# Audio tower on one core: the layer norms' epsilon kept as a 129th column beside the squares, in place of an addition on GpSimd

## The chip, the cores and the metric

The kernel runs on one NeuronCore of one Trainium2 chip, as one program. The metric is the device time of one execution in microseconds; three runs of the kernel before gave 622.33, 622.41 and 625.29, a median of 622.41.

## The reference, cut to what matters

64 recordings of 4000 samples go through seven 1-D convolutions (10 taps with stride 5; four with 3 taps and two with 2 taps, all stride 2), each with 128 channels, a layer norm over the channels and an exact Gelu. A last layer norm and a projection to 192 columns give 12 tokens a recording; attention and a feed-forward part with nine experts follow, each behind a layer norm.

```python
def _fp32_layernorm(x, g, b, eps=1e-05):
    xf = x.astype(jnp.float32)
    mu = xf.mean(-1, keepdims=True)
    var = xf.var(-1, keepdims=True)
    y = (xf - mu) * jax.lax.rsqrt(var + eps) * g.astype(jnp.float32) + b.astype(jnp.float32)
    return y.astype(x.dtype)

h = x[:, None, :]
for w, g, b, s in zip(conv_ws, ln_gs, ln_bs, strides):
    h = _conv1d(h, w, s)
    h = jnp.swapaxes(h, -2, -1)
    h = _fp32_layernorm(h, g, b)
    h = jnp.swapaxes(h, -2, -1)
    h = jax.nn.gelu(h, approximate=False)
```

## The kernel before

The recordings are worked in eight groups of eight (g = 0 to 7). Layers 1 to 6 are cut into 128 blocks ("chunks") of 1 to 4 tiles; a tile is up to 128 positions (partitions) by C = 128 channels (columns), so a full block is 128 x 512 in one PSUM bank. The taps are centred beforehand, so a convolution's output has mean zero over the channels, and the norm needs only the sum of its squares. For block n this is done:

- `conv` (L750, TensorE): the convolution into PSUM bank n mod 3. It waits until the product of block n-3 is done (`xh_done`) and for the Gelus that make its input.
- `square` (L1361, ScalarE): the squares of the block into `sq`, one of two halves of 512 columns of the tile `work`.
- `group` on VectorE (L1080): `ssum`, the sum over each run of 128 columns.
- `group` on GpSimd (L599, L602): `varv` = `ssum` + C times eps, then `rstd` = `varv` to the power -0.5. A semaphore (`varv_done`) stands between the two.
- `norm` (L1090, VectorE): `xh`, in the second half of `work`, is the block in PSUM times `rstd`.
- `turn` (L762, TensorE): transposes of `xh` into one PSUM bank, `tr`, which has to be free of the Gelu before.
- `gelu` (L1379, ScalarE): Gelu with the layer's scale and offset, into the input tiles of the next layer. It writes a block in two runs, or for layer 1 with a step of 13 columns.

Layer 0 is computed otherwise: its variances come from a Gram matrix (`z` jobs, L792 to L796 on TensorE, L1041 to L1046 on VectorE), GpSimd raises them to -0.5 in long pows (L593, `power_first`), VectorE scales the samples and splits them in a high and a low part (`scale`: L1054, L1058, L1060), TensorE transposes and multiplies them (L806, L815), and ScalarE's Gelu (L1390) writes 128 columns into each of four blocks of a ring.

The order is written out by hand. `SLOTS` is a list of slots, each with at most one block, some jobs of layer 0 or of the feed-forward part, pows of layer 0, and steps of the token part (layer norms, attention, routing). Every engine walks through the same slots, and each has its own order within slot k:

- TensorE: conv of block k, turn of block k-2 (`LAG = 2`), jobs, token steps.
- ScalarE: square of block k, gelu of block k-2, Gelus of the jobs, token steps.
- VectorE: norm of block k-1, then group (the sum) of block k, jobs, scaling, token steps.
- GpSimd: group of block k, then long pows, then token steps. A token norm is an addition and a pow on 96 x 1 (L607, L609), whose product on VectorE is L1104 and whose transposes on TensorE are L842 and L843. In the four slots behind the head GpSimd also writes constants (L626 to L672) and starts the clearing of a table in HBM (L650).

The squares wait for the sum of block n-2 before they overwrite its half of `sq`. Behind the last slot come the sorted tokens' experts (L981 to L1005), which the change does not touch. At 2.4 GHz a convolution of a full block of layers 1 to 4 is 12 matmuls, which the profile counts as 24 passes.

Of the kernel before, what the change touches and what calls it, by code (L numbers as in the profile page):

```python
# [8 lines left out]
ALU = mybir.AluOpType  # L9
ACT = mybir.ActivationFunctionType  # L10
X = mybir.AxisListType.X

P = 128
BATCH, SAMPLES = 64, 4000
C = 128
# [10 lines left out]
EPS = 1e-5  # L26
# [25 lines left out]
CUTS = [None, (4, 4, 4, 4, 4, 4, 2), (4, 3, 3, 3), (4, 3), (4,), (2,), (1,)]  # L52
# [220 lines left out]
def audio_tower(nc, a, out):  # L273
    ctx = ExitStack()
    with ctx:
        def sb(name, shape, dt=F32):
            return ctx.enter_context(nc.sbuf_tensor(name, shape, dt))

        def sem(name):
            return ctx.enter_context(nc.semaphore(name))  # L280
# [21 lines left out]
        for l in range(1, 6):  # L302
            n = ODD[l] + EVEN[l]
# [24 lines left out]
        r0 = sb("r0", [1, 3])  # L328
        neghalf = sb("neghalf", [P, 4])
        eps = sb("eps", [P, 1])  # L330
        ceps = sb("ceps", [P, 4])
        work = sb("work", [P, 2048])
        sq = work[:, 0:1024].rearrange("p (b c) -> p b c", b=2)
        xh = work[:, 1024:2048].rearrange("p (b c) -> p b c", b=2)
        ssum = sb("ssum", [P, 4, 4])
        varv = sb("varv", [P, 4, 4])
        rstd = sb("rstd", [P, 4, 4])

        projw = sb("projw", [P, D])
# [75 lines left out]
        def ybank(n):  # L415
            return ps[:, n % 3, :]
# [7 lines left out]
        s_const = sem("s_const")  # L424
# [21 lines left out]
        conv_done = sem("conv_done")  # L446
        sq_done = sem("sq_done")
        ssum_done = sem("ssum_done")
        varv_done = sem("varv_done")
        rstd_done = sem("rstd_done")  # L450
        xh_done = sem("xh_done")
        tr_done = sem("tr_done")
# [109 lines left out]
        def _(gp):  # L562
# [19 lines left out]
            gp.memset(half0[:, :], -0.5).then_inc(s_const, 1)  # L582
            gp.memset(neghalf[:, :], -0.5).then_inc(s_const, 1)
            gp.memset(eps[:, :], EPS).then_inc(s_const, 1)
            gp.memset(ceps[:, :], C * EPS).then_inc(s_const, 1)
            for l in range(4):
                gp.dma_start(lnraw[8 + l:9 + l, :], a[f"L0_tok_ln_b{l}"].rearrange("(a c) -> a c", a=1)).then_inc(s_lnb, 16)
            gp.wait_ge(s_const, 10)
# [6 lines left out]
            def group(n):  # L595
                l, _, k = CHUNKS[n]
                rows, count, idx = ROWS_OF[l], CUTS[l][k], n % 4
                gp.wait_ge(ssum_done, n + 1)
                gp.tensor_tensor(varv[0:rows, idx, 0:count], ssum[0:rows, idx, 0:count], ceps[0:rows, 0:count],  # L599
                                 ALU.add).then_inc(varv_done, 1)  # L600
                gp.wait_ge(varv_done, n + 1)
                gp.tensor_tensor(rstd[0:rows, idx, 0:count], varv[0:rows, idx, 0:count],  # L602
                                 neghalf[0:rows, 0:count], ALU.pow).then_inc(rstd_done, 1)

            def power(tag, r):
# [69 lines left out]
            for k, (chunk, _, prep) in enumerate(SLOTS):  # L675
                if chunk is not None:
                    group(NUMBER[chunk])
                for what, g, i in prep:
                    if what == "pow":
                        power_first(g, i)  # L680
                for step, r in STEPS[k]:
                    tokens(step, r)
                if len(HEAD) <= k < len(HEAD) + 4:
                    constants(k - len(HEAD))
# [27 lines left out]
        def _(pe):  # L712
# [41 lines left out]
            def turn(chunk):  # L754
                n = NUMBER[chunk]
                l, _, k = chunk
                rows, count = ROWS_OF[l], CUTS[l][k]
                pe.wait_ge(xh_done, n + 1)
                if n >= 1:
                    pe.wait_ge(act_done, n)  # L760
                for j in range(count):
                    last = nc.tensor.transpose(tr[:, j * rows:(j + 1) * rows],  # L762
                                               xh[0:rows, n % 2, j * C:(j + 1) * C], ident[0:rows, 0:rows])
                last.then_inc(tr_done, 1)
# [19 lines left out]
            def job_z(job):  # L784
                _, g, part = job
                o = room(job)
                pe.wait_ge(j_dve, DVE_TO[JOB[("raw", g)] + 1])
                pe.wait_ge(s_gram, 1)
                band = gram[:, :, :].rearrange("p w z -> p (w z)")
                full_w = BAND * K0  # L790
                if part == 0:
                    nc.tensor.matmul(o[:, 0:full_w], xwin[:, 0:P], band, start=True, stop=True).then_inc(j_done, 1)  # L792
                else:
                    rest = (LOCALS - 2 * BAND) * K0
                    nc.tensor.matmul(o[:, 0:full_w], xwin[:, P:2 * P], band, start=True, stop=True)
                    nc.tensor.matmul(o[:, full_w:full_w + rest], xwin[:, 2 * P:3 * P], band[:, full_w - rest:full_w],  # L796
                                     start=True, stop=True).then_inc(j_done, 1)

            def job_xt(job):
                _, g, q = job  # L800
                o = room(job)
                pe.wait_ge(s_parts, scales_before(g) + scaled_for(g, q))
                for i in range(min(4, TRIPLES - 4 * q)):
                    tri = 4 * q + i
                    src = xhl[:, 3 * tri:3 * tri + 3, :].rearrange("p l k -> p (l k)")
                    last = nc.tensor.transpose(o[0:12 * K0, i * P:(i + 1) * P], src, ident[:, :])  # L806
                last.then_inc(j_done, 1)
# [214 lines left out]
        def _(ve):  # L1022
# [52 lines left out]
            def group(n):  # L1075
                l, _, k = CHUNKS[n]
                rows, count = ROWS_OF[l], CUTS[l][k]
                w = count * C
                ve.wait_ge(sq_done, n + 1)
                nc.vector.reduce_sum(ssum[0:rows, n % 4, 0:count],  # L1080
                                     sq[0:rows, n % 2, 0:w].rearrange("p (j c) -> p j c", c=C), axis=X).then_inc(ssum_done, 1)

            def norm(n):
                l, _, k = CHUNKS[n]
# [154 lines left out]
            for k, (chunk, jobs, prep) in enumerate(SLOTS):  # L1239
                if k >= 1 and ORDER[k - 1] is not None:  # L1240
                    norm(NUMBER[ORDER[k - 1]])
                if chunk is not None:
                    group(NUMBER[chunk])
                for job in jobs:
                    if job[0] not in ON_ACT and k > 2:
                        WORK[job[0]](job)
                for what, g, i in prep:
                    if what == "xs" and k > 2:
                        scale(g, i)
                for step, r in STEPS[k]:  # L1250
                    tokens(step, r)
                if k == 8:
                    late_pads()
# [12 lines left out]
            count = pa[0:1, 16:16 + NE]  # L1266
# [76 lines left out]
        def _(ac):  # L1343
# [11 lines left out]
            def square(n):  # L1355
                l, _, k = CHUNKS[n]
                rows, w = ROWS_OF[l], CUTS[l][k] * C
                ac.wait_ge(conv_done, n + 1)
                if n >= 2:
                    ac.wait_ge(ssum_done, n - 1)  # L1360
                nc.scalar.activation(sq[0:rows, n % 2, 0:w], ybank(n)[0:rows, 0:w], ACT.Square).then_inc(sq_done, 1)  # L1361

            def gelu(n):
                l, g, k = CHUNKS[n]
# [128 lines left out]
```

## Time and profile before

| | |
|---|---|
| median of 3 runs | 622.41 us |
| the profiled execution's own time | 628.29 us |
| its span | 626.6 us |
| TensorE busy (matmuls) | 572.0 us, 91% |
| weight loads busy | 542.5 us, 87% |
| VectorE busy | 319.8 us, 51% |
| ScalarE busy | 320.0 us, 51% |
| GpSimd busy | 291.6 us, 47% |
| mean clock granted to TensorE, 40 to 80 us | 0.83 |
| the same, 80 to 484 us | 1.00 |
| the same, 500 to 556 us | 0.66 |

The head (loading and the first two groups) reaches to about 110 us, the body of group 2 to 165, those of groups 3 to 6 have a period of 56.5 us, and the last group with the attention of the last tokens ends at 556; the experts take the rest. Times in the text are microseconds from the start of the span. A clock of 1.00 is 2.4 GHz and 0.50 is 1.2 GHz; means lie between. TensorE's busy share is no measure of how near it is to its peak, since the ends of matmuls are modelled; a short wait shows better in the idle time ahead of a weight load (PEld).

### The profile page before, as it was taken

Reading aid. Unit: us, or ns where it says so; the run is one execution under the profiler, and the core shown is the slowest. Engines: PE = TensorE matmul, PEld = TensorE weight load, DVE = VectorE, ACT = ScalarE, POOL = GpSimd, SP = SyncE. Lnnn points to the kernel's source line nnn. Section 1 sums busy time; section 2 is a strip of 40 time slices with the busy share of each in tenths; the row PEclk is TensorE's granted clock in tenths of the full one; section 3 lists DMA queues with packets and bytes.
Section 4 is the critical chain, followed back from the end, with each engine's and each line's share of the span. In section 5 each row is a group of like instructions: output and inputs, shape, how many; then the busy total and the mean of one; then the engine's idle time right before and its main releaser. Section 6 shows DMA issues by size and latency. Waiting matters only on the chain.

```text
span 626.6 us, 11944 instructions
## 1 busy us (share of the span) xinstructions
PE 572.0 (91%) x4499; PEld 542.5 (87%) x4499; DVE 319.8 (51%) x755; ACT 320.0 (51%) x507; POOL 291.6 (47%) x425
## 2 busy tenths in 40 slices
PE   6877899999999998999999999989999977789996
PEld 6777899988989998998999899988898765689995
DVE  4653346356466756756574766555553433341232
ACT  2545456655674656557565656654643413244441
POOL 5573157677429535842764495234333120114433
PEclk9998799999999999999999999999999866699998
DMA  7290000294000000000000000000000094042110
GB/s 180 70 286 9 2 1 10 75 221 108 2 2 1 15 2 1 1 6 1 2 1 7 1 2 6 1 1 1 6 2 6 0 247 119 6 121 59 53 40 10
DMA packets 17523, 26.40 MB, mean 42 GB/s; under 512 B 2172, under 2 KB 13397, under 8 KB 17467
## 3 DMA queue, kind: packets, MB, share of 16 engines
q1 hardware_dynamic: 14155, 15.85, 9.4%
q0 software_dynamic: 3296, 9.78, 6.4%
q8 instruction: 37, 0.61, 0.4%
q14 instruction: 19, 0.16, 0.1%
q10 hardware_dynamic: 16, 0.00, 0.0%
HBM read 17.13 MB, written 9.18 MB: 42 GB/s over the span
## 4 chain that ended last, share of the span: by engine, by line
PE 74%; POOL 8%; ACT 7%; DVE 6%; issue 4%; DMA 1%; SPq 1%; POOLq 0%; DVEq 0%; ACTq 0%
PE ps L750 38%; PE ps L762 5%; PE ps L1005 4%; PE ps L836 3%; PE ps L815 3%; POOL rstd L593 3%; PE ps L994 3%; PE ps L993 3%; POOL rstd L602 2%; ACT h L1390 2%; ACT work L1361 2%; PE ps L876 2%; PE ps L806 2%; ACT wide L1379 2%; PE ps L896 1%
## 5 line engine op out<-in xcount | busy, mean ns | idle before, releaser
L750 PE MATMUL ps<-wt,h 128*128 128x128 f32 x1248 | 155.3, 282 | 10.0 <-ACT h L1390 9.0
L1361 ACT ACTIVATE work<-ps 128x512 f32<-128x512 f32 (+7 forms) x128 | 67.3, 525 | 188.4 <-PE ps L750 188.1
L750 PEld LDWEIGHTS ps<-wt,h 128*128 128x128 f32 x1248 | 150.2, 198 | 11.8 <-issue 6.5
L750 PE MATMUL ps<-wt,wide 128*128 128x128 f32 (+2 forms) x1248 | 150.5, 274 | 5.6 <-ACT wide L1379 5.4
L750 PEld LDWEIGHTS ps<-wt,wide 128*128 128x128 f32 (+2 forms) x1248 | 144.6, 184 | 9.0 <-issue 6.1
L599 POOL TENSOR_TENSOR varv<-ssum,ceps 128x4 f32<-128x4 f32 (+7 forms) x128 | 26.2, 205 | 208.8 <-DVE ssum L1080 208.6
L1080 DVE TENSOR_REDUCE ssum<-work 128x4 f32<-128x512 f32 (+7 forms) x128 | 75.6, 590 | 91.6 <-ACT work L1361 91.5
L602 POOL TENSOR_TENSOR rstd<-varv,neghalf 128x4 f32<-128x4 f32 (+7 forms) x128 | 117.0, 914 | 10.0
L1090 DVE TENSOR_TENSOR work<-ps,rstd 128x512 f32<-128x512 f32 (+7 forms) x128 | 76.4, 597 | 82.8 <-POOL rstd L602 82.7
L1379 ACT ACTIVATE wide<-ps,lncol 128x512 f32<-128x512 f32 (+6 forms) x120 | 109.3, 911 | 2.3 <-PE ps L762 1.6
L593 POOL TENSOR_TENSOR rstd<-var,half 128x10 f32<-128x10 f32 (+2 forms) x39 | 82.8, 2129 | 9.0 <-DVE var L1046 9.0
L1390 ACT ACTIVATE h<-ps,lncol 128x512 f32<-128x512 f32 (+1 forms) x120 | 82.0, 728 | 2.3 <-PE ps L815 2.3
L762 PE MATMUL ps<-ident,work 128*128 128x128 f32 (+2 forms) x424 | 66.9, 272 | 6.5 <-ACT wide L1379 5.5
L762 PEld LDWEIGHTS ps<-ident,work 128*128 128x128 f32 (+2 forms) x424 | 50.2, 143 | 9.1 <-issue 6.9
L815 PE MATMUL ps<-cols,w0t 120*128 120x512 f32 (+1 forms) x120 | 43.4, 424 | 2.1 <-DVE cols L1067 0.8
L1453 ACT ACTIVATE work<-ps 128x768 f32<-128x768 f32 x13 | 10.6, 812 | 34.8 <-PE ps L994 34.7
L1005 PE MATMUL ps<-W2s,work 128*128 x156 | 27.6, 327 | 0.0
L706 POOL DMA_INDIRECT out_dram<-xnat,idt x13 | 13.2, 1013 | 30.3 <-DVE xnat L1318 29.7
L1067 DVE CAST cols<-ps 120x512 fp32r<-120x512 f32 (+1 forms) x40 | 25.1, 628 | 1.5 <-PE ps L806 1.5
L1005 PEld LDWEIGHTS ps<-W2s,work 128*128 128x128 f32 x156 | 25.1, 190 | 0.3 <-issue 0.3
L607 POOL TENSOR_TENSOR veps<-mv,eps 96x1 f32<-96x1 f32 x24 | 5.1, 214 | 42.2 <-DVE mv L1100 42.1
L1301 DVE COPY xst<-ps 96x256 f32<-96x256 f32 x13 | 5.5, 421 | 37.3 <-issue 26.9
(218 smaller groups left out, 756.4 us busy)
## 6 DMA issues: line engine op xcount, KB each, us to landing
sorted_tokens<-zero POOLq DMA_DIRECT2D x1, 5886.5 KB, 31.6
W2s<-in_L_ffn_W_dram SPq DMA_DIRECT2D x9, 576.0 KB, 8.7
wide<-in_L_ffn_W_dram SPq DMA_DIRECT2D x8, 576.0 KB
cols<-sorted_tokens SPq DMA_DIRECT2D x13, 96.5 KB, 1.9
xnat<-in_x_dram SPq DMA_DIRECT2D x7, 135.0 KB
wt<-in_L_ffn_b_dram SPq DMA_DIRECT2D x1, 864.0 KB, 4.2
wide<-in_L_tok_conv_w_dram SPq DMA_DIRECT2D x4, 192.0 KB, 3.5
common_sums<-acc POOLq DMA_DIRECT2D x1, 579.0 KB, 5.7
```

The source lines that it names most:

```text
L593: gp.tensor_tensor(rstd0[:, lo:hi], var0[:, lo:hi], half0[:, lo:hi], ALU.pow).then_inc(s_pow, 1)
L599: gp.tensor_tensor(varv[0:rows, idx, 0:count], ssum[0:rows, idx, 0:count], ceps[0:rows, 0:count], ALU.add).then_inc(varv_done, 1)
L602: gp.tensor_tensor(rstd[0:rows, idx, 0:count], varv[0:rows, idx, 0:count], neghalf[0:rows, 0:count], ALU.pow).then_inc(rstd_done, 1)
L750: last = nc.tensor.matmul(y[0:rows, j * C:(j + 1) * C], src, wt[:, TAP0[l] + tap, :], start=(tap == 0), stop=(tap == taps - 1))
L762: last = nc.tensor.transpose(tr[:, j * rows:(j + 1) * rows], xh[0:rows, n % 2, j * C:(j + 1) * C], ident[0:rows, 0:rows])
L815: nc.tensor.matmul(o[:, 0:w], w0t[:, j, :], xcol[q % 2][0:12 * K0, 0:w], start=True, stop=True).then_inc(j_done, 1)
L1005: last = nc.tensor.matmul(o, ht[:, b, f * P:(f + 1) * P], W2s[:, bass.ds(own, 1), f, :].rearrange("p e d -> p (e d)"), start=(f == 0), sto ...
L1080: nc.vector.reduce_sum(ssum[0:rows, n % 4, 0:count], sq[0:rows, n % 2, 0:w].rearrange("p (j c) -> p j c", c=C), axis=X).then_inc(ssum_done, 1)
L1090: nc.vector.tensor_tensor(xh[0:rows, n % 2, 0:w].rearrange("p (j c) -> p j c", c=C), ybank(n)[0:rows, 0:w].rearrange("p (j c) -> p j c", c=C),
L1361: nc.scalar.activation(sq[0:rows, n % 2, 0:w], ybank(n)[0:rows, 0:w], ACT.Square).then_inc(sq_done, 1)
L1379: nc.scalar.activation(dst, src, ACT.Gelu, bias=lncol[:, 8 + l:9 + l], scale=lncol[:, l:l + 1]).then_inc(act_done, 1)
L1390: nc.scalar.activation(dst, src, ACT.Gelu, bias=lncol[:, 8:9], scale=lncol[:, 0:1]).then_inc(j_act, 1)
```

## The change

`work` grows from 2048 to 8 x 129 + 1024 = 2056 columns. Its first part is now `sq` with four dimensions: two halves, four tiles, 129 columns. The 129th column of each tile is set once, at the start, to C times eps. Square writes 128 columns of each tile and leaves the 129th; the sum on VectorE reads all 129, so `ssum` already has C times eps in it. GpSimd's addition and its wait go, and its pow reads `ssum`. The tiles `ceps` and `varv` and one semaphore go.

```diff
-        ceps = sb("ceps", [P, 4])
-        work = sb("work", [P, 2048])
-        sq = work[:, 0:1024].rearrange("p (b c) -> p b c", b=2)
-        xh = work[:, 1024:2048].rearrange("p (b c) -> p b c", b=2)
+        work = sb("work", [P, 8 * (C + 1) + 1024])
+        sq = work[:, 0:8 * (C + 1)].rearrange("p (b j c) -> p b j c", b=2, c=C + 1)
+        xh = work[:, 8 * (C + 1):].rearrange("p (b c) -> p b c", b=2)
...
-        varv = sb("varv", [P, 4, 4])
...
-            gp.memset(ceps[:, :], C * EPS).then_inc(s_const, 1)
+            gp.memset(sq[:, :, :, C:C + 1], C * EPS).then_inc(s_const, 1)
...
                 gp.wait_ge(ssum_done, n + 1)
-                gp.tensor_tensor(varv[0:rows, idx, 0:count], ssum[0:rows, idx, 0:count], ceps[0:rows, 0:count],
-                                 ALU.add).then_inc(varv_done, 1)
-                gp.wait_ge(varv_done, n + 1)
-                gp.tensor_tensor(rstd[0:rows, idx, 0:count], varv[0:rows, idx, 0:count],
+                gp.tensor_tensor(rstd[0:rows, idx, 0:count], ssum[0:rows, idx, 0:count],
                                  neghalf[0:rows, 0:count], ALU.pow).then_inc(rstd_done, 1)
...
-                nc.vector.reduce_sum(ssum[0:rows, n % 4, 0:count],
-                                     sq[0:rows, n % 2, 0:w].rearrange("p (j c) -> p j c", c=C), axis=X).then_inc(ssum_done, 1)
+                nc.vector.reduce_sum(ssum[0:rows, n % 4, 0:count], sq[0:rows, n % 2, 0:count, :], axis=X).then_inc(ssum_done, 1)
...
-                nc.scalar.activation(sq[0:rows, n % 2, 0:w], ybank(n)[0:rows, 0:w], ACT.Square).then_inc(sq_done, 1)
+                nc.scalar.activation(sq[0:rows, n % 2, 0:CUTS[l][k], 0:C], ybank(n)[0:rows, 0:w].rearrange("p (j c) -> p j c", c=C),
+                                     ACT.Square).then_inc(sq_done, 1)
```

## Rows read from the trace of the kernel before

**Rows 1.** Page: the chain by line, then groups (busy, mean ns, idle before).
```profile
PE ps L750 38%; PE ps L762 5%; PE ps L1005 4%; PE ps L836 3%; PE ps L815 3%; POOL rstd L593 3%; PE ps L994 3%; PE ps L993 3%; POOL rstd L602 2%; ACT h L1390 2%; ACT work L1361 2%; PE ps L876 2%; PE ps L806 2%; ACT wide L1379 2%; PE ps L896 1%
...
L599 POOL TENSOR_TENSOR varv<-ssum,ceps 128x4 f32<-128x4 f32 (+7 forms) x128 | 26.2, 205 | 208.8 <-DVE ssum L1080 208.6
...
L602 POOL TENSOR_TENSOR rstd<-varv,neghalf 128x4 f32<-128x4 f32 (+7 forms) x128 | 117.0, 914 | 10.0
```

**Rows 2.** Chain that ended last, in order of time: start, us, what.
```profile
112.47 0.21 POOL varv L599
...
142.20 0.16 POOL varv L599
...
171.47 2.68 PE ps L750 x24
```

**Rows 3.** Timeline of all engines, head: start, us, instruction, idle before and releaser.
```profile
37.85 0.77 ACT L1390 ACTIVATE h<-ps,lncol 128x512 f32<-128x512 f32 x1
37.98 0.69 DVE L1090 TENSOR_TENSOR work<-ps,rstd 128x512 f32<-128x512 f32 x1 [2.88 <-POOL rstd L602]
...
38.77 1.47 PE L750 MATMUL ps<-wt,h 128*128 128x128 f32 x11 [0.99 <-DVE work L1090]
```

**Rows 4.** Timeline, head: TensorE behind ScalarE's Gelus.
```profile
44.83 4.43 PE L750 MATMUL ps<-wt,h 128*128 128x128 f32 x24 [2.35 <-ACT h L1390]
```

**Rows 5.** Timeline of TensorE's weight loads, body of group 2.
```profile
127.32 0.19 PEld L815 LDWEIGHTS ps<-cols,w0t 120*128 120x128 f32 x1 [0.26 <-DVE xwin L1034]
...
128.86 0.31 PEld L762 LDWEIGHTS ps<-ident,work 128*128 128x128 f32 x3 [0.37 <-DVE work L1090]
...
141.06 0.42 PEld L762 LDWEIGHTS ps<-ident,work 128*128 128x128 f32 x4 [0.46 <-DVE work L1090]
...
145.47 0.41 PEld L806 LDWEIGHTS ps<-ident,xhl 128*120 128x120 f32 x4 [1.14 <-issue]
```

**Rows 6.** Timeline of all engines, body of group 2.
```profile
131.69 0.49 ACT L1361 ACTIVATE work<-ps 128x384 f32<-128x384 f32 x1 [0.89 <-PE ps L750]
...
134.53 4.50 POOL L593 TENSOR_TENSOR rstd<-var,half 128x12 f32<-128x12 f32 x2
...
142.95 1.97 POOL L593 TENSOR_TENSOR rstd<-var,half 128x10 f32<-128x10 f32 x1
...
144.25 0.41 DVE L1058 CAST xhl<-xsc 128x480 fp32r<-128x480 f32 x1
...
144.70 0.66 DVE L1060 TENSOR_TENSOR xhl<-xsc,xhl 128x480 fp32r<-128x480 f32 x1
```

**Rows 7.** Timeline of TensorE's weight loads, group 3 and the last group.
```profile
240.19 0.31 PEld L762 LDWEIGHTS ps<-ident,work 128*128 128x128 f32 x3 [1.16 <-issue]
...
258.34 0.12 PEld L842 LDWEIGHTS ps<-ident,xn 96*96 96x96 f32 x1 [0.23 <-DVE xn L1104]
...
478.19 0.12 PEld L842 LDWEIGHTS ps<-ident,xn 96*96 96x96 f32 x1 [1.25 <-DVE xn L1104]
```

**Rows 8.** One line's instructions, L609: duration in ns, least, median, most.
```profile
L609 POOL TENSOR_TENSOR rs<-veps,neghalf x24: 542/550/989, 152.8 to 540.0; 96x1 f32<-96x1 f32 x24
```

**Rows 9.** Timeline of all engines around the token pow of group 3.
```profile
255.90 0.40 DVE L1054 TENSOR_TENSOR xsc<-xnat,rstd 128x240 f32<-128x240 f32 x1
...
256.80 0.66 DVE L1060 TENSOR_TENSOR xhl<-xsc,xhl 128x480 fp32r<-128x480 f32 x1
256.88 0.99 POOL L609 TENSOR_TENSOR rs<-veps,neghalf 96x1 f32<-96x1 f32 x1
```

**Rows 10.** Groups by line and shape: busy, mean ns of one, idle before.
```profile
L1390 ACT ACTIVATE h<-ps,lncol 128x512 f32<-128x512 f32 x96 | 69.8, 770 | 2.3 <-PE ps L815 2.3
L1379 ACT ACTIVATE wide<-ps,lncol 128x512 f32<-128x512 f32 x56 | 65.9, 1177 | 0.7 <-PE ps L762 0.5
...
L1080 DVE TENSOR_REDUCE ssum<-work 128x4 f32<-128x512 f32 x56 | 38.3, 684 | 66.7 <-ACT work L1361 66.7
```

**Rows 11.** Timeline of all engines, group 3: a Gelu of layer 2.
```profile
239.30 0.78 ACT L1379 ACTIVATE wide<-ps,lncol 128x512 f32<-128x512 f32 x1
```

More of the change, by code:

```diff
@@ L448, in audio_tower @@
         ssum_done = sem("ssum_done")
-        varv_done = sem("varv_done")
         rstd_done = sem("rstd_done")
@@ L1077, in group @@
                 rows, count = ROWS_OF[l], CUTS[l][k]
-                w = count * C
                 ve.wait_ge(sq_done, n + 1)
-                nc.vector.reduce_sum(ssum[0:rows, n % 4, 0:count],
-                                     sq[0:rows, n % 2, 0:w].rearrange("p (j c) -> p j c", c=C), axis=X).then_inc(ssum_done, 1)
+                nc.vector.reduce_sum(ssum[0:rows, n % 4, 0:count], sq[0:rows, n % 2, 0:count, :], axis=X).then_inc(ssum_done, 1)
             def norm(n):
```

## The prediction

> **What bounds the kernel now.** I read the page's busy shares first, then the chain that ended last, by line and piece by piece, then TensorE's own idle time, taken on its weight loads (the modelled ends of matmuls hide short gaps, the weight loads show them), and last the timeline around each gap. TensorE is busy 91% and its convolutions head the chain; the pow on GpSimd (L602) has 2% and the addition ahead of it (L599) is under the lines listed [rows 1]. A block goes convolution (PE), Square (ACT), sum (DVE), addition and pow (POOL), product (DVE), transposes (PE), Gelu (ACT). TensorE transposes block k-2 after convolving block k, so two slots cover this path. DVE multiplies block k-1 before it sums block k, so where POOL is late the next sum is late too, and POOL and DVE run as a loop. The reader should look for the places where TensorE waits for something that comes out of that loop.
>
> **What goes.** 128 additions of 0.205 us, each followed by about 0.08 us before the pow starts (10.0 us over 128) [rows 1]: 26.2 + 10.0 = 36 us of GpSimd's time, 0.28 us a block; where pow already queues behind other GpSimd work it is 0.24. Nearly all of it lies beside TensorE's work. The chain holds 16 additions: two in the head, ten in one unbroken run from 112.47 to 142.20 [rows 2], three at 188 to 197 and one at 475.
>
> *The head.* The run into 38.77 has two additions, at 28.5 and 36.7, so the pow's product would end 0.5 us earlier, and TensorE idles 0.99 us there for it [rows 3]. But this convolution also needs the Gelu that ACT runs from 37.85 to 38.62, behind a Square that TensorE itself released; the product ends at 38.67 [rows 3]. The second wait ends 0.05 us before the first. Gain: 0.05, taken as nothing. The later gaps of the head are ACT's own (44.83: 2.35 us for Gelus) [rows 4].
>
> *The body of group 2, 125 to 146.* Here GpSimd also writes constants, and its queue is late until 146. TensorE's weight loads idle 0.26, 0.37, 0.46 and 1.14 us [rows 5], together 2.23, each for a DVE result that sits behind the loop. Replayed without additions: the queue is 1.1 us ahead at 124 and 1.3 at 127, so the first two gaps go, and TensorE is 0.6 earlier. From there the lead is cut, since the sum that opens the pair of long pows waits for the Square at 131.69, which TensorE releases [rows 6]: 131.69 - 0.60 + 0.49 + 0.03 = 131.6, sum 0.55, wait 0.07, pow 0.85, then the variance that DVE has ready by then, gives a pair start of 133.2 for 134.53, 1.35 early. Two more additions, at 139.0 and 142.2, go at 0.24 each, so the product behind the last comes 1.8 early; the third gap goes whole (TensorE 1.06 early). The DVE steps behind it keep their lengths, and the high and low parts (L1060), done at 145.36 [rows 6], are done at 143.6. TensorE's transposes then start at 143.75 for 145.47: 1.7 us gained, with 0.46 of the last gap left. Bounds: 0.8 (another wait takes half) and 2.2 (all four gaps). I take 1.7.
>
> *Groups 3 to 6.* The period is 56.5 us, and its large gaps are ACT's: 1.16 at 240.19 [rows 7], behind two table loads, Squares and a Gelu, and 0.8 us near 250, where a Gelu stands behind a Square. No addition is in them. Once a period, though, TensorE waits for the normalized tokens: 0.30, 0.23, 0.23, 0.23 us at 201.89, 258.34, 314.81, 371.25 (one row stands) [rows 7]. That wait hangs on the token pow (L609), which takes 0.99 us here and 0.55 elsewhere [rows 8]: it starts at 256.88, while DVE's L1060, with two operands in SBUF, runs to 257.46, and ends 0.41 behind it [rows 9]. Three additions lie ahead of it in GpSimd's queue. Part of the first one's 0.28 is lost, since the long pow's variance is ready only then, so 0.14 + 0.27 + 0.24 = 0.65 is its lead. It would be asked for at 256.2 and done before 256.95; the product then follows L1060 at 257.5, is done at 257.9, and TensorE, which has its previous transposes until 258.1, does not wait. Gain 0.2 to 0.3 each, 0.9 in the four.
>
> The Trainium skill, page "SBUF — State Buffer", section "Who interferes with whom", says that a VectorE instruction with two SBUF inputs and a GpSimd one that reads SBUF exclude one another, and that the first to issue blocks the other for its whole length. The 0.99 agrees with it; taken whole it speaks against this change, as rival 1 works out.
>
> *The last groups.* At 478.19 TensorE idles 1.25 us for a token pow that stands directly behind a block's addition and pow [rows 7]: 0.25 gained. Elsewhere after 407 the gaps come from token steps, tables or DVE's order; nothing.
>
> **What is added.** The sum reads up to 4 kept columns more: 684 ns for 512 columns is 1.3 ns a column at most [rows 10], 5 ns a block, 0.05 us over the dozen sums on the chain. Square writes up to four runs of 128 with a gap of one column, and reads as before. No such Square is in the trace. The nearest row is the Gelu of L1390, which writes four runs of 128 columns, far apart, in 770 ns [rows 10]; the Gelu of L1379 at 239.30 writes two runs of 256 in 0.78 [rows 11]. Twice the runs, the same time: 0. On the other side stands the L1379 form whose mean is 1177 ns, because its writes of layer 1 step over 13 columns [rows 10]: 0.4 us more. A cost below nothing is excluded for both, since no element less is read or written. I take 0, since runs of 128 are what Square writes; the far end is rival 4. One constant is written to 8 columns in place of 4 during loading, with the same count of signals: nothing. Tensors behind `work` move by 48 bytes; I take 0. No DMA, queue or wait is added; in each engine's fixed order, what comes earlier can only be late again through a longer instruction.
>
> **The sum.** 1.7 + 0.9 + 0.25 - 0.05 = 2.8 us. The profiled execution took 628.29 (span 626.6), 5.9 more than the median of the runs, 622.41; 625.5 against 628.29, and taken off the median 619.6, 0.45%.
>
> **Rivals.**
> 1. *The pow gets in the way of DVE.* Asked for 0.65 earlier, the token pow meets L1054 (to 256.30) and would start ahead of L1058 [rows 9]. If it held DVE off for its 0.55, L1058 and L1060 would end at 257.95 for 257.46, the transposes that need them start at 258.05 for 257.65, and the token transpose at 258.5 for 258.34: 0.2 lost a body in place of 0.2 gained, 1.7 - 0.8 + 0.25 = 1.15 gained, 621.3. If it simply finds L1060 again it gains nothing: 620.5. Against it: a long pow ran from 142.95 to 144.92 with L1058 (0.41) inside it and L1060 across its end, at 0.66 as at 256.80 [rows 6, 9]; a pow in its middle holds nothing. That it needs the port at its start speaks for it. By the rule of "SBUF — State Buffer" in the Trainium skill it would be 621.3.
> 2. *The clock changes sides.* After a gap of 2.35 us, 24 matmul passes at 1.2 GHz took 4.43 us [rows 4]; the same 24 take 2.68 at 2.4 GHz [rows 2]. The head's low stretches lie ahead of the first gain, but those of the last groups (mean clock 0.66 from 500 to 556, in the table) will meet TensorE's work 2.8 us displaced. One stretch fewer is 1.5 us: 618.1; one more: 621.1.
> 3. *TensorE's work is the whole bound.* The gaps on GpSimd's side are replaced at once by ACT's, as in the head, and only 0.3 is left: 622.1. For it: 38.77. Against it: at 141.06 and 145.47 the Gelus were long done.
> 4. *Square becomes longer, the kernel slower.* Squares have 2% of the chain, 12.5 us [rows 1], some 22 to 25 of about 0.5 us; both ACT gaps of each period have one in them. With 0.4 us more each the cost is 22 x 0.4 = 8.8, less 2.8 gained: 628.4. It decides from 0.13 us a Square (no change) and from 0.27 (slower by 0.5%).
>
> **How the numbers follow.** Forecast 0.50 (own range 618.4 to 620.7); rival 1 0.17; rival 2 0.18, two thirds of it on the fast side; rival 3 0.09; rival 4 0.06. About 0.5% is what a measurement of this kernel can tell from no change: that is 619.3 and 625.5. The forecast lies 0.3 us from that line, so 0.24 of its 0.50 is beyond it; with rival 2's fast side, 0.12, faster has 0.36. Slower has rival 4, 0.06; the rest is 0.58. The range from 617.3 to 622.4 takes in all but the far ends of rivals 2 and 4.
>
> **What would show it.** No L599; the pow waits for the sum directly, with unchanged 0.85 and 1.01. TensorE's four gaps between 127 and 146 shrink to one of about 0.5. The wait before L842 disappears in four bodies, with L609 back near 0.55 to 0.7; if it is still 0.99, or L1058 and L1060 are longer, rival 1 holds. The gap at 38.77 stays but names ACT. The period of 56.5 us shortens by 0.2. Square stays at 598 ns and the sum rises to 688; a Square above 0.7 would make the prediction wrong, as would a group 2 body whose last gap stays over 1 us.

## The result

The changed kernel takes 620.34 us in the median of 22 runs (617.1 to 625.84), the kernel before 622.39 in 22 runs beside them (620.05 to 627.84): a ratio of 0.996, 95% interval 0.9941 to 0.9979. A second set of 12 runs gave 619.96 beside 622.89 for 35 runs of before, and 0.9964 (0.9932 to 0.9996). So it is 2 to 3 us faster, 0.4%, near the 2.8 us of the prediction's sum; yet its trace shows a gain of over 4 us. That has to be explained.

The page of the changed kernel (span 617.3 us, its own time 619.07), with busy time and share of each engine, the chain by engine and by line, and the groups of the touched lines. Its lines have moved: L602 is now L597, L1361 is L1354, L1080 is L1074, L1090 is L1083, L609 is L604.

```profile
PE 563.6 (91%) x4499; PEld 537.4 (87%) x4499; DVE 319.7 (52%) x755; ACT 319.3 (52%) x507; POOL 264.2 (43%) x297
...
PE 81%; ACT 8%; DVE 4%; issue 3%; POOL 2%; DMA 1%; SPq 1%; POOLq 0%; DVEq 0%; ACTq 0%
...
L597 POOL TENSOR_TENSOR rstd<-ssum,neghalf 128x4 f32<-128x4 f32 (+7 forms) x128 | 117.7, 919 | 235.4 <-DVE ssum L1074 235.2
L1354 ACT ACTIVATE work<-ps 128x512 f32<-128x512 f32 (+7 forms) x128 | 67.3, 526 | 183.0 <-PE ps L745 182.7
...
L1074 DVE TENSOR_REDUCE ssum<-work 128x4 f32<-128x516 f32 (+7 forms) x128 | 76.2, 595 | 114.9 <-ACT work L1354 114.8
```

128 GpSimd instructions are gone and 27.4 us of its busy time; GpSimd has 2% of the chain. The pow waits for the sum directly and is as long as it was (914 ns then [rows 1], 919 now). Taken by shape, a Square of 512 columns stays at 598 ns and the sum of 512 columns goes from 684 [rows 10] to 690.

Where the time went is seen by putting the 128 Squares of ScalarE side by side, the first of one trace with the first of the other, since every block has one and their order doesn't change. Between the twelfth (81.79 us in before) and the last but one (495.40) TensorE is granted its full clock in both, by windows of 5 us up to 495. This stretch took 413.61 us before and 409.47 after: 4.14 us less. By place it went like this, read off the same comparison (a wait of TensorE shows in a Square some us behind it):

| place in before | what was lost there | less by |
|---|---|---|
| 82 to 129 | nothing | 0.0 |
| 129 to 148.13, group 2 | the four gaps of [rows 5] | 1.72 |
| 148.49, behind group 2 | the first gap of L815 | 0.23 |
| groups 3 to 6, one token wait each (L842) and one of L815 each | 0.54, 0.45, 0.49, 0.45 | 1.93 |
| 478.19 | the last token pow | 0.26 |

Below are weight loads of TensorE in after, in the body of group 2 and near 250 us; in brackets is the idle time before one and what ended it. These are all that waited 0.15 us or more from 119 to 146 and from 244 to 262:

```profile
133.68 0.48 PEld L745 LDWEIGHTS ps<-wt,wide 128*104 128x104 f32 x4 [1.01 <-issue]
...
141.04 0.41 PEld L801 LDWEIGHTS ps<-ident,xhl 128*120 128x120 f32 x4 [0.38 <-issue]
...
244.85 0.48 PEld L745 LDWEIGHTS ps<-wt,wide 128*104 128x104 f32 x4 [0.80 <-issue]
```

The four gaps of [rows 5] have shrunk to the 0.38 at 141.04; the 1.01 at 133.68 stood in before too, at 136.86 and as long. The token wait of [rows 7] is not there, and neither is a gap that the prediction never spoke of. In before it stands once in each body from group 2 on, at 148.49, 204.70, 261.14, 317.61 and 374.05, with 0.20 to 0.25 us. The timeline of before around the third:

```profile
259.19 0.69 DVE L1090 TENSOR_TENSOR work<-ps,rstd 128x512 f32<-128x512 f32 x1 [0.91 <-POOL rstd L602]
259.80 0.68 DVE L1080 TENSOR_REDUCE ssum<-work 120x4 f32<-120x512 f32 x1
260.39 0.68 DVE L1067 CAST cols<-ps 120x512 fp32r<-120x512 f32 x1
...
261.14 0.31 PEld L815 LDWEIGHTS ps<-cols,w0t 120*128 120x128 f32 x2 [0.25 <-issue]
```

The profile names "issue", but the load reads `cols`, whose copy ends at 261.07. VectorE makes that copy behind the product and the sum of the slot, and the product had waited 0.91 us for the pow. That the gap hangs on this order is tested below, by moving the copy.

### The profile page after: what moved, and what is told of

Read it like the earlier page. It is cut to its first block, busy times and chain, and to the rows that moved or that the text cites. A ratio compares the mean times of both kernels' runs of the same rounds, so it can differ in the third digit from the quotient of the medians.

```text
span 617.3 us, 11816 instructions
## 1 busy us (share of the span) xinstructions
PE 563.6 (91%) x4499; PEld 537.4 (87%) x4499; DVE 319.7 (52%) x755; ACT 319.3 (52%) x507; POOL 264.2 (43%) x297
## 4 chain that ended last, share of the span: by engine, by line
PE 81%; ACT 8%; DVE 4%; issue 3%; POOL 2%; DMA 1%; SPq 1%; POOLq 0%; DVEq 0%; ACTq 0%
PE ps L745 43%; PE ps L757 6%; PE ps L1000 4%; PE ps L810 3%; PE ps L831 3%; PE ps L989 3%; PE ps L988 3%; ACT h L1384 2%; PE ps L801 2%; ACT wide L1373 2%; PE ps L871 2%; ACT work L1354 2%; PE ps L891 2%; PE ps L879 1%; PE ps L821 1%
## 5 line engine op out<-in xcount | busy, mean ns | idle before, releaser
L597 POOL TENSOR_TENSOR rstd<-ssum,neghalf 128x4 f32<-128x4 f32 (+7 forms) x128 | 117.7, 919 | 235.4 <-DVE ssum L1074 235.2
L1354 ACT ACTIVATE work<-ps 128x512 f32<-128x512 f32 (+7 forms) x128 | 67.3, 526 | 183.0 <-PE ps L745 182.7
L745 PE MATMUL ps<-wt,h 128*128 128x128 f32 x1248 | 152.8, 280 | 10.0 <-ACT h L1384 10.0
L745 PEld LDWEIGHTS ps<-wt,h 128*128 128x128 f32 x1248 | 148.0, 196 | 11.8 <-issue 6.5
L1074 DVE TENSOR_REDUCE ssum<-work 128x4 f32<-128x516 f32 (+7 forms) x128 | 76.2, 595 | 114.9 <-ACT work L1354 114.8
L1083 DVE TENSOR_TENSOR work<-ps,rstd 128x512 f32<-128x512 f32 (+7 forms) x128 | 76.1, 595 | 54.2 <-POOL rstd L597 51.8
L831 PE MATMUL ps<-W2s,h 128*96 128x192 f32 x96 | 23.4, 410 | 0.4 <-ACT h L1390 0.4
L602 POOL TENSOR_TENSOR veps<-mv,eps 96x1 f32<-96x1 f32 x24 | 4.5, 190 | 44.6 <-DVE mv L1093 44.5
```

The costliest lines, as they stand in the source:

```text
L597: gp.tensor_tensor(rstd[0:rows, idx, 0:count], ssum[0:rows, idx, 0:count], neghalf[0:rows, 0:count], ALU.pow).then_inc(rstd_done, 1)
L745: last = nc.tensor.matmul(y[0:rows, j * C:(j + 1) * C], src, wt[:, TAP0[l] + tap, :], start=(tap == 0), stop=(tap == taps - 1))
L831: last = nc.tensor.matmul(o[0:M, 0:D], hc[:, f, i * M:(i + 1) * M], W2s[:, 0, f, :], start=(f == 0), stop=(f == NF - 1))
L1074: nc.vector.reduce_sum(ssum[0:rows, n % 4, 0:count], sq[0:rows, n % 2, 0:count, :], axis=X).then_inc(ssum_done, 1)
L1083: nc.vector.tensor_tensor(xh[0:rows, n % 2, 0:w].rearrange("p (j c) -> p j c", c=C), ybank(n)[0:rows, 0:w].rearrange("p (j c) -> p j c", c=C),
L1354: nc.scalar.activation(sq[0:rows, n % 2, 0:CUTS[l][k], 0:C], ybank(n)[0:rows, 0:w].rearrange("p (j c) -> p j c", c=C), ACT.Square).then_in ...
```

## Why the medians show less than the traces

The runs of one kernel spread over 5 to 9 us, and most of this spread goes with TensorE's clock. Each run lists its span and its mean granted clock; twice the share that is missing to 1.00, times the span, is the time spent at 1.2 GHz. A straight line fitted to the 89 runs of before that list a clock (time against time at 1.2 GHz) has a slope of 0.35 us a microsecond, one through the 34 of after 0.36, and single runs lie some 0.5 us off the line. At equal clock the two kernels are well apart:

| mean clock of the run | before, with the two kernels below that equal it in time: median (runs) | after, both sets: median (runs) |
|---|---|---|
| 0.957 | 626.82 (5) | 622.51 (2) |
| 0.965 | 623.24 (29) | 618.76 (4) |
| 0.968 | 621.99 (20) | 617.49 (5) |

That is 4.3 to 4.5 us, near the 4.14 us of the traced stretch. But the two are not granted the same clock. The mean time at 1.2 GHz is 42.5 us over the 89 runs of before and 49.2 over the 34 of after, 6.7 more (95% interval 4.1 to 9.3), worth 2.4 us. So 4.5 gained less 2.4 given back is the 2.1 us by which the means of the runs differ.

That the change itself brings all of the 6.7 us is not shown. Two kernels below equal before in the stretch, before run again and the one with the column and the addition; their 24 runs had a mean of 45.2 us, 2.6 more than the 89 (0.2 to 5.0). Against those 24, after has 4.1 us more (0.8 to 7.3), worth 1.4.

The traces show where TensorE is at 1.2 GHz: between 20 and 75 us, from about 490 to 560, and for a few us from 610 on; nowhere between. Windows of three executions, TensorE alone (length; busy, count; granted clock; DMA share; GB/s), before:

```profile
40.00:80.00 40.00, 31.01 (x205) 0.83 0.16 45
480.00:560.00 80.00, 63.81 (x344) 0.74 0.33 85
```

after:

```profile
40.00:80.00 40.00, 30.61 (x227) 0.91 0.15 43
480.00:560.00 80.00, 63.47 (x360) 0.79 0.39 104
```

and after once more, in the second set (span 624.5):

```profile
40.00:80.00 40.00, 30.26 (x209) 0.87 0.20 59
480.00:560.00 80.00, 63.81 (x331) 0.72 0.35 92
```

The same program has 0.79 and 0.72 in its tail from one execution to the next, so one profile against one profile tells nothing of the clock, and only the runs together do. In every experiment below I therefore give, beside the medians, the stretch between the two Squares and the time read off the line through the kernel's own runs at 40 us of 1.2 GHz (called its line); for before that is 622.1. Set against before, the line and the stretch agree within 0.6 us, so the line is the coarser of the two.

## The experiments

Theory A, after the first comparison: 4.1 us come from waits of TensorE that GpSimd's queue sets, 1.7 in group 2's body and 0.5 in each later one; layout, Square and sum are worth nothing. Rivals: the layout of the squares gains or costs by itself, the gains of the places depend on each other, or the first trace was a lucky one.

**The kernel before, run again**, to see how far the measure repeats.

> The kernel before, unchanged, for the clock. Theory A (the change takes about 4.1 us out of the part from 80 to 495 us, and the medians show less only because the low-clock stretches of the tail fall differently from run to run): the part from the Square at 81.8 to the one at 495.4 is again 413.6 us, and over the single runs time falls as the mean granted clock rises, some 0.4 us for each us at 1.2 GHz; at a clock of 0.953 the runs are near 626, where those of the changed kernel are near 622. Theory B (the profile shows more than there is): that part differs from run to run by a microsecond or more, and at equal clock the two kernels differ by about 2 us.

623.5 us (12 runs) for 622.72, ratio 1.0022 (0.9997 to 1.0046). The stretch is 413.45 for 413.61 and the line reads 622.0 for 622.1. A stretch repeats to some 0.2 us, while medians of 12 runs can stand 0.8 apart.

**The kept column, with the addition left in.**

```
-            gp.memset(ceps[:, :], C * EPS).then_inc(s_const, 1)
+            gp.memset(sq[:, :, :, C:C + 1], 0.0).then_inc(s_const, 1)
+            gp.memset(ceps[:, :], C * EPS).then_inc(s_more, 1)
...
-                nc.vector.reduce_sum(ssum[0:rows, n % 4, 0:count],
-                                     sq[0:rows, n % 2, 0:w].rearrange("p (j c) -> p j c", c=C), axis=X).then_inc(ssum_done, 1)
+                nc.vector.reduce_sum(ssum[0:rows, n % 4, 0:count], sq[0:rows, n % 2, 0:count, :], axis=X).then_inc(ssum_done, 1)
```

> The squares beside a kept column, which holds zero here, and GpSimd's addition kept: the layout alone. Theory A (the addition is all that counts): the part from the Square at 82 to that at 495 stays at 413.6, at most 0.2 longer, Square 598 ns, sum 688 ns. Rival (the layout or the moved addresses carry part of it): that part is over 0.5 us shorter or longer.

(The lines are shown against before; the Square is that of the change.) 623.58 us, ratio 1.0026 (1.0004 to 1.0048), which the unchanged kernel's 1.0022 beside the same runs matches; stretch 413.66, line 622.0. Square's runs of 128, the sum's 516 columns and the moved tensors together come to 0.05 us in the stretch. The half of the change that had no row in before costs nothing in the stretch, and all that was gained there comes from the addition.

**A second addition ahead of each pow.**

```
+                gp.tensor_tensor(varw[0:rows, idx, 0:count], varv[0:rows, idx, 0:count], zeps[0:rows, 0:count],
+                                 ALU.add).then_inc(varv_done, 1)
+                gp.wait_ge(varv_done, 2 * n + 2)
...
+                gp.tensor_tensor(rstd[0:rows, idx, 0:count], varw[0:rows, idx, 0:count],
```

> Two additions in place of one, the second of zero. Theory A (a chain through GpSimd and VectorE that is barely ahead of TensorE): one more costs more than one less gains, since no slack is left: 0.5 in the head (38.8), 2 to 2.5 in the body of group 2, 0.8 to 1.0 in each of four bodies, 0.3 near 478, so 6 to 8 us, of it 5.5 to 7.5 between the Squares at 82 and 495. Rival (a fixed price): 4.1 us, as much as one less gained. Rival (the gain came from GpSimd's port being free for VectorE): under 3 us.

632.17 us (6 runs), ratio 1.0158 (1.0114 to 1.0203); stretch 421.39, 7.78 more than before and above the 5.5 to 7.5 expected; line 629.8. By place: 1.83 between 82 and 127, where the first addition costs nothing and the expectation had no cost, 2.40 in and just behind group 2, about 0.8 in each later body, 0.27 at 478. The token wait and the L815 gap near 204 us (L850 and L823 here) have both grown:

```profile
202.60 0.12 PEld L850 LDWEIGHTS ps<-ident,xn 96*96 96x96 f32 x1 [0.68 <-DVE xn L1112]
205.67 0.31 PEld L823 LDWEIGHTS ps<-cols,w0t 120*128 120x128 f32 x2 [0.52 <-issue]
```

In before they were 0.30 and 0.25. One addition fewer gives 4.1 and one more costs 7.8: the price of 0.28 us on this queue rises as its slack is used up, and the slack differs from place to place. No price per instruction would have given either number.

**The change, with additions (of zero, since the column holds the epsilon) in group 2's body alone.**

```
+BODY2 = range(NUMBER[(1, 2, 0)], NUMBER[(1, 3, 0)])
+def ADDED(n):
+    return n in BODY2
...
+                if ADDED(n):
+                    added[0] += 1
+                    gp.tensor_tensor(varv[0:rows, idx, 0:count], ssum[0:rows, idx, 0:count], ceps[0:rows, 0:count],
+                                     ALU.add).then_inc(varv_done, 1)
+                    gp.wait_ge(varv_done, added[0])
+                    src = varv
```

> The changed kernel with the addition (of zero) kept in the 16 blocks of group 2's body alone. Theory A (the gain is made in two places that do not touch): the part from 82 to 495 is 411.4, that is 2.2 under before and 1.9 over the changed kernel. Rival (group 2's lateness is carried into the later bodies): the later bodies keep part of their gaps, and it is 412.5 or more.

619.83 us, ratio 0.9955 (0.9928 to 0.9981); stretch 411.35, 2.26 less than before, line 619.5. Group 2's gaps are those of before; here are its last and the first of L815:

```profile
142.83 0.41 PEld L822 LDWEIGHTS ps<-ident,xhl 128*120 128x120 f32 x4 [1.15 <-issue]
145.85 0.31 PEld L831 LDWEIGHTS ps<-cols,w0t 120*128 120x128 f32 x2 [0.20 <-issue]
```

**Its complement: additions everywhere but there** (`return n not in BODY2`).

> The changed kernel with GpSimd's addition (of zero) kept in front of every block's pow but those of group 2's body: the complement of the run with additions in that body alone. Theory A (the gains of group 2 and of the later bodies stand beside one another and add up): stretch from the Square at 81.79 to that at 495.40 411.7 us (1.94 less than before: 1.71 in group 2 and 0.23 behind it), and all of it between 125 and 152; the token transposition waits of 0.23 and the waits of 0.20 to 0.25 at 204.70 and its like are there again; read at equal time at 1.2 GHz 2.0 us below before. Theory B (the pow in body 2 gains only because GpSimd came there earlier out of the head's queue, so additions ahead of it take part of it away): stretch 412.3 or more.

623.04 us, ratio 0.9969 (0.9942 to 0.9996). Stretch 411.62, 1.99 less, all of it between 129 and 152, line 620.2. It and the kernel ahead of it sum to 2.26 + 1.99 = 4.25 for the 4.14 of the whole. The places are independent to 0.1 us, as theory A has it. Its median alone, above that of before (622.89), would have said that the change in group 2 does nothing; its 12 runs had a mean of 45.0 us at 1.2 GHz.

**The change once more.**

> The changed kernel once more, unedited, beside the runs of the kernel before on the same chip. From the Square at 81.79 to that at 495.40 (place in the order of Squares) the first trace of after had 409.47 us against 413.61 of before, 4.14 less, while the medians differ by 2.05. Theory A (4.1 to 4.5 us are gained in every run, and the medians show less because TensorE is granted 1.2 GHz about 3 us longer in the runs of after, at 0.34 us of time for each such us): stretch 409.5 again, median 620.3 (619.5 to 621.5), and a line through time against time at 1.2 GHz, read at 40 us, gives 617.6 for it and 622.1 for before. Theory B (the first trace of after was a lucky one, and the gain is the 2 us of the medians): the stretch is above 410.8, and the lines at 40 us stand 2 to 3 us apart.

619.96 us; stretch 409.47, the same to 0.01 us, line 617.65. The first trace was no lucky one. The extra time at 1.2 GHz over the runs beside it is 7 us (2 to 12), rather than the 3 that I had taken from the medians of the first sets.

**Group 2's constants earlier, in the changed kernel and in before.** GpSimd writes constants in four slots of that group; here four slots that lie 13 earlier.

```
-                if len(HEAD) <= k < len(HEAD) + 4:
-                    constants(k - len(HEAD))
+                if 12 <= k < 16:
+                    constants(k - 12)
```

> The changed kernel with four pieces of GpSimd's constant writing moved from four slots of group 2 to four slots 13 slots earlier, where GpSimd's queue is short. Theory A (what makes group 2 unlike groups 3 to 6 is that GpSimd's own queue is late there, and the gap of 0.38 us left at 141 in after is the rest of it): that gap goes, stretch 409.0 us (0.4 to 0.6 below after), and nothing is lost in the head, median 0.3 to 0.6 below after's on the same chip. Theory B (the rest at 141 is DVE's own order, which GpSimd does not set): the gap stays within 0.1, stretch 409.3 to 409.6.

> The kernel before, addition kept, with the same four pieces moved. Theory A (the 1.9 us between 125 and 152 come from additions met by a late GpSimd queue): without the lateness body 2 loses only what the other bodies lose, 0.5, so 1.4 to 1.9 us go: stretch 411.8 to 412.2 for 413.6, and the change on top of it (the run before this one) is worth 2.9 rather than 4.1 us. Theory B (the addition costs body 2 its 1.9 us wherever the constants are written): stretch 413.4 or more.

On after: 621.2 us, ratio 0.9965 (0.9939 to 0.9991) to before, stretch 409.43, line 617.5, and the gap is where it was:

```profile
142.79 0.41 PEld L801 LDWEIGHTS ps<-ident,xhl 128*120 128x120 f32 x4 [0.38 <-issue]
```

So theory A of this pair is wrong here: the constants are not what is left. The chain of after, in order of time, says what is (start, length, instruction):

```profile
128.51 0.50 ACT work L1354
...
130.64 4.50 POOL rstd L591 x2
135.14 0.97 POOL rstd L597
136.11 1.92 POOL rstd L591
138.03 0.52 POOL rstd L597
```

From 130.64 to 138.55 GpSimd works through the next group's long pows and the blocks' own without a break, and the chain runs through that series. That it sets what is left is read from the chain; no run here shortens it. On before, the same move gave stretch 412.55, 1.06 less, line 620.4, median 623.61 (ratio 1.0005, 0.9975 to 1.0036). Three of the gaps of [rows 5] go and the last is left, with one of L815:

```profile
144.60 0.41 PEld L806 LDWEIGHTS ps<-ident,xhl 128*120 128x120 f32 x4 [1.05 <-issue]
147.62 0.31 PEld L815 LDWEIGHTS ps<-cols,w0t 120*128 120x128 f32 x2 [0.20 <-issue]
```

It falls between the two theories. About 1.1 us of what the additions cost in group 2 they cost only because the constants had made the queue late; the rest is still there with the constants away, and by the chain it comes through the series of long pows. Behind this move the change is worth 412.55 - 409.43 = 3.1 us, not 4.1.

**The copy to `cols` ahead of the product**, in the bodies from group 2 on, in before and in after, to see whether the five gaps that the prediction lacked come from the copy's place in VectorE's order.

```
+                first = [job for job in jobs if k >= len(HEAD) and job[0] == "xt" and job[2] == 0]
+                for job in first:
+                    job_xt(job)
                 if k >= 1 and ORDER[k - 1] is not None:
                     norm(NUMBER[ORDER[k - 1]])
...
-                    if job[0] not in ON_ACT and k > 2:
+                    if job[0] not in ON_ACT and k > 2 and job not in first:
```

> The kernel before, addition kept; in each body of groups 2 to 6 VectorE copies the first columns of the next group (the copy to cols, 0.68 us, ahead of TensorE's gaps of 0.20 to 0.25 us at 148.49, 204.70, 261.14, 317.61 and 374.05) ahead of the product that waits for the block's pow, not behind it; its source is done by 201.9 and VectorE idles there until 202.74. Theory A (those five gaps come from GpSimd's queue by way of the product and the sum ahead of the copy; they are the part of the change's gain that the prediction lacked): the five gaps go, stretch from the Square at 81.79 to that at 495.40 412.4 us for 413.6 (1.0 to 1.25 less), the gaps of 0.23 at 258.34 and its like stay. Theory B (the gaps are TensorE's own order or an issue cost, as the profile names them): they stay, stretch 413.4 or more.

> The same move of the copy in the changed kernel, where the gaps at 204.70 and its like are gone already. Theory A (without the addition the copy is in time): nothing is left to gain, stretch 409.4 to 409.5 as in after. Theory B (the copy is late still and only hidden): 409.2 or less.

On before: stretch 412.16, 1.45 less, line 620.6; steps of 0.23 to 0.28 at each of the five places, 1.34 in all, and another 0.1 spread between them, while the token waits stay:

```profile
254.96 0.13 PEld L842 LDWEIGHTS ps<-ident,xn 96*96 96x96 f32 x1 [0.22 <-DVE xn L1104]
```

The expected 1.0 to 1.25 was a little short. On after: stretch 409.38, nothing, as expected. The move of the copy ends the five gaps with every addition in place, and taking the additions out ends them with the copy in place. Hence they were a wait for GpSimd by way of VectorE's order, and the change removes them whole. The medians, 623.43 (ratio 1.0019, 0.9988 to 1.005) and 621.12 (0.9976, 0.9942 to 1.001), can't show a step of this size.

**The token's pow ahead of the long pow**, in before, in four slots.

```
+                ahead = [(step, r) for step, r in STEPS[k] if k >= len(HEAD) and step[:5] == "power"]
+                for step, r in ahead:
+                    tokens(step, r)
                 for what, g, i in prep:
                     if what == "pow":
                         power_first(g, i)
                 for step, r in STEPS[k]:
-                    tokens(step, r)
+                    if (step, r) not in ahead:
+                        tokens(step, r)
```

> The kernel before, addition kept; in four slots (of groups 3 to 6) GpSimd makes the token's addition and pow (L607, L609) ahead of the long pow of 1.96 us and not behind it; its variance is there at 197.13, as GpSimd starts on the block. Theory A (TensorE's four waits of 0.23 to 0.30 at 201.89, 258.34, 314.81 and 371.25 hang on this pow's place in the queue, and the gaps at 204.70 and its like on the queue's end): the four waits go; the queue's end comes earlier only by what the pow loses of its 0.99 us, 0.15 to 0.4, so the later gap grows from 0.25 to between 0.1 and 0.35, and the stretch is 412.4 to 413.0 us for 413.6. Theory B (the waits have another cause): stretch 413.5 or more. The pow itself: 0.55 to 0.7 us for 0.99 by theory A, as it no longer meets L1060.

622.47 us (ratio 1.0013, 0.9976 to 1.005); stretch 411.64, 1.97 less, line 619.6. That is more than the 0.6 to 1.2 expected: both waits of groups 3 to 6 are gone, 0.49 us a body, with every addition still there. GpSimd's timeline at the first of the four:

```profile
195.49 0.19 POOL L607 TENSOR_TENSOR veps<-mv,eps 96x1 f32<-96x1 f32 x1
195.75 0.55 POOL L609 TENSOR_TENSOR rs<-veps,neghalf 96x1 f32<-96x1 f32 x1
196.27 1.96 POOL L593 TENSOR_TENSOR rstd<-var,half 128x10 f32<-128x10 f32 x1
198.20 0.29 POOL L599 TENSOR_TENSOR varv<-ssum,ceps 128x4 f32<-128x4 f32 x1
```

and that of before at the same place:

```profile
199.95 0.34 POOL L607 TENSOR_TENSOR veps<-mv,eps 96x1 f32<-96x1 f32 x1
200.37 0.99 POOL L609 TENSOR_TENSOR rs<-veps,neghalf 96x1 f32<-96x1 f32 x1
201.32 0.19 POOL L599 TENSOR_TENSOR varv<-ssum,ceps 128x4 f32<-128x4 f32 x1
```

Where the token's two instructions don't meet VectorE's L1054 to L1060 they take 0.74 us instead of 1.33. The 0.59 is twice what an addition with its gap costs, and it ends both waits at once. In groups 3 to 6, then, there is one cause with two symptoms: the queue was some 0.25 us late at two points, and either way of taking 0.5 to 0.65 us off it, the additions or the stretched pow, brings it in time at both.

No kernel here beats after beyond the measure: the constants earlier and the copy first read 617.5 and 617.6 on the line for its 617.65.

## Why the prediction held, step by step

*The median*, 619.6 predicted for 620.34, is right by 0.7 us, and this closeness is luck: 2.8 was put where the traces have 4.14, and nothing was put for the clock, which took 2.4 back. The two errors nearly cancel. The mechanism, TensorE waiting at a few places for results behind GpSimd's queue, was right.

*The head, 0.* Right at the place that it worked out, with its reason. Six of the first seven Squares, up to 51.63 us in before, stand the same 0.17 to 0.19 us earlier in after (the sixth 0.06), so nothing was gained there; from there to 81.79 the two clocks differ, and no trace compares. TensorE still idles 0.99 us, and the wait now names ScalarE; for [rows 3] after has

```profile
38.59 1.58 PE L745 MATMUL ps<-wt,h 128*128 128x128 f32 x12 [0.99 <-ACT h L1384]
```

*Group 2, 1.7.* 1.72 in the trace and 1.99 with the first L815 gap behind it when done alone. On the way TensorE was 0.45 and then 0.94 us earlier, for 0.6 and 1.06 in the replay, and the last step was larger than its 0.64, so part of the match is luck. The pair of long pows started at 130.64, which is 133.37 in before's time, 1.2 us early for the 1.35 of the replay. The replay also gave what is left of the last gap, 0.46 predicted for 0.38. What it did not say is that 1.1 us of this hangs on the constants.

*Groups 3 to 6, 0.9.* This is the term that was mis-sized: 1.93, and 0.23 more behind group 2. The waits of L842 were found and sized right, 0.2 to 0.3 each, and the token pow came where the replay had put it. After is 5.39 us ahead of before there, so its start at 250.87 is 256.26 in before's time, for the 256.2 of the replay:

```profile
250.71 0.40 DVE L1049 TENSOR_TENSOR xsc<-xnat,rstd 128x240 f32<-128x240 f32 x1
250.87 0.72 POOL L604 TENSOR_TENSOR rs<-veps,neghalf 96x1 f32<-96x1 f32 x1
251.14 0.41 DVE L1053 CAST xhl<-xsc 128x480 fp32r<-128x480 f32 x1
...
251.59 0.66 DVE L1055 TENSOR_TENSOR xhl<-xsc,xhl 128x480 fp32r<-128x480 f32 x1
```

The step that failed is "once a period, though, TensorE waits for the normalized tokens": it waits twice. I took the second gap, which the profile gives to "issue", as TensorE's own and didn't look at what its weights read. The period was to shorten by 0.2 us and did by 0.45 to 0.49.

*The last group, 0.25.* 0.26, and of the 1.25 us at 478.19 this is left:

```profile
471.32 0.12 PEld L837 LDWEIGHTS ps<-ident,xn 96*96 96x96 f32 x1 [0.99 <-DVE xn L1097]
```

*Square, sum, layout, 0 and 5 ns a block.* Right: 598 ns, 684 to 690, and 0.05 us in the stretch for all of it with the addition left in.

*Rival 1, the pow gets in DVE's way.* False. L1053 and L1055 keep their 0.41 and 0.66, above, for 0.41 and 0.66 in [rows 6, 9]. It is the pow that gets longer where it starts under one of them: 0.72 for 0.55 beside L1049, and at 140.45, in group 2, the block's pow takes 1.34 for 1.01 beside L1055. No wait of TensorE of 0.15 us or more follows that pow before 154. The rows of after:

```profile
138.51 1.97 POOL L591 TENSOR_TENSOR rstd<-var,half 128x10 f32<-128x10 f32 x1
139.38 0.40 DVE L1049 TENSOR_TENSOR xsc<-xnat,rstd 128x240 f32<-128x240 f32 x1
...
140.26 0.66 DVE L1055 TENSOR_TENSOR xhl<-xsc,xhl 128x480 fp32r<-128x480 f32 x1
140.45 1.34 POOL L597 TENSOR_TENSOR rstd<-ssum,neghalf 128x4 f32<-128x4 f32 x1
```

The Trainium skill, page "SBUF — State Buffer", section "Who interferes with whom", says that a VectorE instruction with two SBUF inputs and a GpSimd one that reads SBUF contend. The traces agree as far as a pow that starts under such an instruction is concerned, 0.99 against 0.55; they don't bear out that whichever issued first holds the other off for its whole length, which the section says in its line on two-port modes: the long pow of 1.97 us above runs over L1049, and L1055 starts under its end, and they stay at 0.40 and 0.66.

*Rival 2, the clock changes sides.* This one happened, on its slow side, and beside a larger gain, as far as the runs can tell the change's share from the rest. It had been priced at 1.5 us for one stretch, where its own rows give 4.43 - 2.68 = 1.75; over the runs it was 2.4, or 1.4 against the 24 runs of the two equal kernels. I gave the fast side two thirds of it without a reason from the rows.

*Rival 3, TensorE's work is the whole bound*, and *rival 4, a longer Square*: false, the first by the 4.14 us of the stretch, the second by the Square's 598 ns.

What stays open is why the changed kernel's runs have 6.7 us more at 1.2 GHz, and how much of it is the change's. It is not simply the size of the displacement: the kernel with additions in group 2 alone, 2.3 us ahead of before in the stretch, had a mean of 42.3 us, no more than before's 42.5, while before with the constants earlier, only 1.1 ahead and with every addition in place, had 50.4, more than after's 49.2.

## What to carry to other kernels

A small instruction on a queue is worth what the lateness of the queue makes it worth: the same 0.28 us cost nothing at the wait in the head and 0.5 us a body in groups 3 to 6, and a second one cost 0.8 a body more. Before pricing it, list every gap of the bounding engine, those named "issue" among them, look up which tile the waiting load reads, and follow that tile's writer back through the order of its engine. Where the clock moves a run by more than the change does, compare runs at equal clock, and a stretch at full clock in the trace, before believing a difference of medians; then ask separately whether the change alters the clock.

## What the runs showed beyond that

- The time of a run follows its granted clock closely, 0.35 to 0.36 us for each us at 1.2 GHz over the runs of before and of after, and goes from 617.1 to 626.97 us for one program. A stretch at full clock repeats to 0.01 to 0.2 us.
- An activation that writes four runs of 128 columns a column apart takes the 598 ns of one that writes 512 in a row.
- A GpSimd pow of 96 x 1 takes 0.55 us alone, 0.72 and 0.99 where it starts under VectorE instructions with two SBUF operands. Additions stretch too: a token's takes 0.19 us alone, 0.34 beside L1058 in before, and 0.53 beside the product of L1060 in the kernel with two additions, as does a block's at 144.89 in before.
- The five gaps that the profile names "issue" ahead of the weight loads of L815 were waits for VectorE's copy: moving the copy ended all five, with the additions in place.
